# A routed attention and expert kernel: destination column written once, four row buffers, query mask on ACT, keys and context remainder fused on DVE

## What is computed

```python
x = x + xattn(layernorm(x), ctx)      # 16 heads of 16, keys and values from ctx; blocks of 64 queries see their own 64 keys
x = x + ffn(layernorm(x))

def ffn(x):
    weights = softmax(x @ gate_w.T + expert_bias)          # 8 experts
    top_w, top_i = top_k(weights, 2); top_w = top_w / (sum(top_w) + 1e-6)
    out = sum over e of sparse_w[e] * (gelu(x @ w_up[e].T) @ w_down[e].T)      # width 1024
    return layernorm(out) + x
```

## Time and profile before

| What | us |
|---|---|
| median of 3 runs | 847.35 (847.29 to 849.61) |
| the profiled execution, its time | 847.34 |
| its span, first to last instruction | 845.5 |
| outside the span | 1.84 |

### The profile page before, as it was taken

One profiled execution on the slowest core, in us unless ns is written; L12 is line 12 of the kernel. 1 busy time (PEld: TensorE's weight loads), 2 busy tenths in 40 slices (PEclk: granted clock), 3 DMA queues, 4 the chain that ended last, 5 costly groups with the idle time before them and its releaser, 6 DMA issues.

```text
span 845.5 us, 19594 instructions
## 1 busy us (share of the span) xinstructions
PE 731.7 (87%) x6084; PEld 661.2 (78%) x6084; DVE 568.6 (67%) x1356; ACT 355.6 (42%) x651; POOL 408.2 (48%) x629
## 2 busy tenths in 40 slices
PE   4999999989899883059659999999999999999990
PEld 4899999889788873048548999999989889999980
DVE  4899999999989983068145555555666667766662
ACT  2777777667566651022112222222333334433441
POOL 3676776557688876644363111111233335433353
PEclk9999999999999997569888999999999999999995
DMA  4333333233345433443742111112222233333222
GB/s 157 101 101 103 111 104 113 88 88 107 125 132 144 125 100 112 122 133 103 194 124 85 51 51 50 39 48 69 82 88 88 82 93 105 107 95 94 83 89 93
DMA packets 61785, 84.17 MB, mean 100 GB/s; under 512 B 7232, under 2 KB 52672, under 8 KB 61696
## 3 DMA queue, kind: packets, MB, share of 16 engines
q1 hardware_dynamic: 54016, 62.98, 25.8%
q0 software_dynamic: 6816, 18.65, 6.1%
q10 hardware_dynamic: 864, 1.36, 0.5%
HBM read 53.56 MB, written 29.40 MB: 98 GB/s over the span
## 4 chain that ended last, share of the span: by engine, by line
PE 41%; issue 23%; POOL 20%; DVE 7%; DMA 5%; SPq 2%; ACT 0%; POOLq 0%; DVEq 0%; ACTq 0%
PE ps_a L578 11%; PE ps_b L594 10%; POOL y_rows L1176 6%; POOL x_sorted L1100 4%; PE ps_a L453 4%; PE ps_b L496 3%; PE ps_a L533 2%; PE ps_c L475 2%; PE ps_c L480 2%; POOL tiny L1163 2%; PE ps_b L463 2%; DMA x_sorted<-area,slot_row 2%; PE ps_a L518 2%; POOL weights_s L1144 1%; DMA area<-xn_rows 1%
## 5 line engine op out<-in xcount | busy, mean ns | idle before, releaser
L578 PE MATMUL ps_a<-area,weights_s 128*128 128x256 f16 x1872 | 217.3, 277 | 1.6 <-DVE area L909 1.6
L594 PE MATMUL ps_b<-weights_s,area 128*128 x1872 | 210.6, 273 | 0.6 <-issue 0.6
L578 PEld LDWEIGHTS ps_a<-area,weights_s 128*128 x1872 | 185.8, 99 | 26.3 <-issue 2.8
L594 PEld LDWEIGHTS ps_b<-weights_s,area 128*128 128x128 f16 x1872 | 183.1, 98 | 22.1 <-issue 0.9
L1176 POOL DMA_INDIRECT y_rows<-weights_s,tiny x78 | 85.7, 1099 | 128.6 <-ACT weights_s L1065 100.9
L1058 ACT ACTIVATE area<-ps_a 128x512 f32<-128x512 f32 x156 | 92.6, 597 | 119.7 <-PE ps_a L578 119.0
L945 DVE SCALAR_TENSOR_TENSOR area<-area 128x512 f16<-128x512 f32 x156 | 108.1, 693 | 5.3
L1065 ACT ACTIVATE weights_s<-ps_b 128x512 f32<-128x512 f32 x39 | 23.3, 599 | 197.5 <-PE ps_b L594 165.4
L1100 POOL DMA_INDIRECT x_sorted<-area,slot_row x64 | 69.5, 1087 | 63.3 <-POOL area L1096 45.8
L943 DVE TENSOR_SCALAR area<-area 128x512 f16<-128x512 f32 x156 | 67.2, 430 | 23.6 <-ACT area L1058 22.5
L907 DVE TENSOR_SCALAR area<-ps_c 128x512 f16<-128x512 f32 x39 | 26.9, 689 | 79.1 <-PE ps_c L561 78.9
(11 more groups left out here) (149 smaller groups left out, 1158.3 us busy)
## 6 DMA issues: line engine op xcount, KB each, us to landing
weights_s<-weights SPq DMA_DIRECT2D x32, 512.0 KB, 3.6
area<-x_sorted SPq DMA_DIRECT2D x39, 257.0 KB, 2.9
area<-xn_rows SPq DMA_DIRECT2D x64, 128.0 KB, 2.5
area<-y_rows SPq DMA_DIRECT2D x32, 256.0 KB, 2.9
resid<-x_in SPq DMA_DIRECT2D x32, 128.0 KB, 2.2
area<-ctx_t SPq DMA_DIRECT2D x32, 128.0 KB, 2.0
xn_rows<-area SPq DMA_DIRECT2D x32, 128.0 KB, 1.7
out<-resid SPq DMA_DIRECT2D x32, 128.0 KB, 2.8
```

The source lines that it names most:

```text
L578: mm = pe.matmul(ps_h[:, q, (ic % 2) * SLOTS:(ic % 2 + 1) * SLOTS], weights_s[:, bass.ds(first + ((2 * hc + part) * WCOLS + ic * P), P)], ...
L594: mm = pe.matmul(ps_y[:, b, v * D:(v + 1) * D], g[b][:, ic, v * P:(v + 1) * P], weights_s[:, bass.ds(first + (col + part * WCOLS), D)], st ...
```

## The change

The destination column is no longer written into each buffer by POOL. `xn_rows` becomes twice 4096 rows of 257 columns; its last column is filled once from a constant by one DMA on ACT's queue at the start; SP stores each tile's rows twice; a row load brings all 257 columns. POOL's scatter waits for the load alone. There are four row buffers, and `spill` is read from the constants. The distribution of the scatters over the steps is new: one tile each in steps 22 to 34 (0 to 12), two each in steps 35 and 36 (13 to 16); tiles 17 to 21 come after the steps on POOL, and on SP after item 2.

The query operand is written by ACT out of PSUM with mask as scale and masked bias as bias, in four operations of 128 x 128, behind L1010 and ahead of the exponential; `q_b` is gone. The key operand is written by DVE in two fused operations over all 128 partitions with a strip mask, which wait for the four query operations; the zeros at the start are gone. The context's remainder is one fused DVE operation behind the keys, and the scaling of the context goes into ACT's rounding operation and into this one.

```diff
-RING = 3
+RING = 4
...
+    r[:, R_AT:R_END] = SLOTS + p[:, None] + P * np.arange(TOPK * TILES)[None]
...
-        xn_rows = nc.dram_tensor("xn_rows", [TOKENS, D], F32, kind="Internal").ap()
+        xn_rows = nc.dram_tensor("xn_rows", [TOPK * TOKENS, ROW], F32, kind="Internal").ap()
...
-            if i < 32:
+            if i < 35:
                 return (i - 22,)
-            return (10,) if i == 32 else (2 * i - 55, 2 * i - 54)
+            return (2 * i - 57, 2 * i - 56)
...
             def row_in(n):
                 for m, s, uses in loads_of(n):
                     since(sp, rsc[s], 16 * uses)
+                    if m == 0:
+                        sp.wait_ge(at_out, 16)
                     sp.wait_ge(xn2_out[n % 2], 16 * (n // 2 + 1))
-                    sp.dma_start(xr[s][:, 0:D], xn_rows[n * P:(n + 1) * P, :]).then_inc(rin[s], 16)
+                    sp.dma_start(xr[s], xn_by_tile[n + m % TOPK * TILES]).then_inc(rin[s], 16)
...
-                    sp.dma_start(xn_rows[bass.ds(t * P, P), :], xn2).then_inc(xn2_out[b], 16)
+                    sp.dma_start(xn_by_tile.rearrange("(c t) p d -> t p c d", c=TOPK)[bass.ds(t, 1), :, :, 0:D].rearrange("a p c d -> p (a c) d"),
+                                 xn2.unsqueeze(1).to_broadcast([P, TOPK, D])).then_inc(xn2_out[b], 16)
...
-                for n in {-3: (19, 20, 21), -1: (22, 23), 0: (24, 25, 26), 1: (27, 28, 29, 30, 31)}.get(k, ()):
+                for n in {-2: (17, 18, 19, 20, 21), -1: (22, 23), 0: (24, 25, 26), 1: (27, 28, 29, 30, 31)}.get(k, ()):
                     row_in(n)
...
-                    pe.wait_ge(q_r, t + 1)
-                    pe.wait_ge(k_r, STRIPS * (t + 1))
+                    pe.wait_ge(q_r, 2 * HC * (t + 1))
+                    pe.wait_ge(k_r, HC * (t + 1))
...
-                                           k_bd[:, c, n].rearrange("p s k -> p (s k)"), start=True, stop=True)
+                                           k_bd[:, c, :, n * BLOCK:(n + 1) * BLOCK], start=True, stop=True)
...
-            dve.memset(k_bd.rearrange("p c b s k -> p (c b s k)"), 0.0).then_inc(zeroed, 1)
...
                 t, half, b = here(j, u, 1)
                 if valid(t):
                     dve.wait_ge(k_ps, t + 1)
-                    since(dve, q_r, t)
-                    dve.tensor_tensor(q_b, ps_q, bq_s.unsqueeze(2).to_broadcast([P, HC, P]), ALU.add).then_inc(qb_r, 1)
-                    for s in range(STRIPS):
-                        r = slice(32 * s, 32 * s + 32)
-                        dve.tensor_tensor(k_bd[r, :, :, s, :], ps_k[r].rearrange("p c (b k) -> p c b k", b=NB),
-                                          bk_s[r].unsqueeze(2).unsqueeze(3).to_broadcast([32, HC, NB, BLOCK]), ALU.add).then_inc(k_r, 1)
+                    dve.wait_ge(q_r, 2 * HC * (t + 1))
+                    since(dve, s_ps, t)
+                    for c in range(HC):
+                        dve.scalar_tensor_tensor(k_bd[:, c], ps_k[:, c].unsqueeze(1).to_broadcast([P, SIDE, P]), bk_s[:, c:c + 1],
+                                                 cst[:, C_STRIP:C_STRIP + SIDE].unsqueeze(2).to_broadcast([P, SIDE, P]),
+                                                 ALU.add, ALU.mult).then_inc(k_r, 1)
+
+                t, half, b = here(j, u, 0)
+                if valid(t):
+                    dve.wait_ge(ctx_hi_r, t + 1)
+                    since(dve, v_ps, t)
+                    dve.scalar_tensor_tensor(ctx_lo, ctx[b], CTX_SCALE, ctx_hi, ALU.mult, ALU.subtract).then_inc(ctx_lo_r, 1)
...
-            act.dma_start(rc, route_consts).then_inc(rc_in, 16)
+            act.dma_start(rc, route_consts[:, 0:R_AT]).then_inc(rc_in, 16)
+            act.dma_start(xn_rows.rearrange("(g p) d -> p g d", p=P)[:, :, D:ROW], route_consts[:, R_AT:R_END].unsqueeze(2),
+                          allow_slow_non_contiguous=True).then_inc(at_out, 16)
...
-                    act.wait_ge(ctx_in[b], 16 * (half + 1))
-                    act.wait_ge(k_ps, t + 1)
-                    act.activation(ctx[b], ctx[b], ACT.Copy, scale=CTX_SCALE).then_inc(ctx_scaled, 1)
...
-                    act.wait_ge(ctx_scaled, t + 1)
+                    act.wait_ge(ctx_in[b], 16 * (half + 1))
                     since(act, v_ps, t)
-                    since(act, ctx_lo_r, t)
-                    act.activation(ctx_hi, ctx[b], ACT.Copy).then_inc(ctx_hi_r, 1)
+                    act.activation(ctx_hi, ctx[b], ACT.Copy, scale=CTX_SCALE).then_inc(ctx_hi_r, 1)
...
+                t, half, b = here(j, u, 1)
+                if valid(t):
+                    if isinstance(t, int) and t == 0:
+                        act.wait_ge(bqm_r, 1)
+                    act.wait_ge(k_ps, t + 1)
+                    since(act, s_ps, t)
+                    for c in range(HC):
+                        for h in range(2):
+                            act.activation(q_m[:, c, :, h, :], ps_q[:, c].rearrange("p (b q) -> p b q", b=NB), ACT.Identity,
+                                           bias=bq_m[:, c, h:h + 1], scale=cst[:, C_MASK + h:C_MASK + h + 1]).then_inc(q_r, 1)
...
                 for m, s, uses in loads_of(n):
-                    since(pool, rsc[s], 16 * uses)
-                    pool.tensor_scalar(xr[s][:, D:ROW], rc[:, R_P1:R_P1 + 1], float(SLOTS - 1 + n * P + m % TOPK * TOKENS), None,
-                                       ALU.add).then_inc(col_r, 1)
                     pool.wait_ge(rin[s], 16 * (uses + 1))
-                    pool.wait_ge(col_r, m + 1)
...
-                    pool.tensor_tensor(ctx_lo, ctx[b], ctx_hi, ALU.subtract).then_inc(ctx_lo_r, 1)
...
-                    pool.tensor_tensor(q_m.rearrange("p c b h q -> p (c b) h q"),
...
```

More of the change, by code:

```diff
@@ L30 @@
 STRIPS = 4
+SIDE = STRIPS
 NB = P // BLOCK
@@ L73, in constants @@
     c[:, C_MASK:C_MASK + 2] = (p[:, None] // DK % 2) == np.arange(2)[None]
+    c[:, C_STRIP:C_STRIP + SIDE] = (p[:, None] // (2 * DK) % SIDE) == np.arange(SIDE)[None]
     halves = lambda v: np.ascontiguousarray(v.astype(np.float16)).view(np.float32)
@@ L117, in program @@
         gate_bias = cst[:, C_GATE_B:C_END]
-        AREA = 10415
+        AREA = 10416
         area = sb("area", [P, AREA])
@@ L184, in program @@
         item_col = carve(1)
[L185 removed]
+        rc = carve(R_AT)
         tri16, ones16 = (rc[:, n:n + P // 2].bitcast(F16) for n in (R_TRI, R_ONES))
+        spill = rc[:, R_SPILL:R_SPILL + SUBS]
         r_desc, r_row, r_item = (rc[:, n:n + E] for n in (R_DESC, R_ROW, R_ITEM))
@@ L252, in program @@
         xt_ps, xt_r = sem("xt_ps"), sem("xt_r")
-        wv_scaled, wv_hi_r, wv_lo_r, ctx_scaled, ctx_hi_r, ctx_lo_r = (
-            sem(n) for n in ("wv_scaled", "wv_hi_r", "wv_lo_r", "ctx_scaled", "ctx_hi_r", "ctx_lo_r"))
-        q_r, qb_r, k_ps, k_r, v_ps, v_r = (sem(n) for n in ("q_r", "qb_r", "k_ps", "k_r", "v_ps", "v_r"))
+        wv_scaled, wv_hi_r, wv_lo_r, ctx_hi_r, ctx_lo_r = (
+            sem(n) for n in ("wv_scaled", "wv_hi_r", "wv_lo_r", "ctx_hi_r", "ctx_lo_r"))
+        bqm_r, q_r, k_ps, k_r, v_ps, v_r = (sem(n) for n in ("bqm_r", "q_r", "k_ps", "k_r", "v_ps", "v_r"))
         s_ps, max_r, sub_r, p_r, pt_ps, pt_r = (sem(n) for n in ("s_ps", "max_r", "sub_r", "p_r", "pt_ps", "pt_r"))
@@ L354, in _ @@
         def _(sp):
+            xn_by_tile = xn_rows.rearrange("(g p) d -> g p d", p=P)
             def row_in(n):
@@ L470, in step @@
                     pe.wait_ge(xt_r, t + 1)
-                    since(pe, qb_r, t)
-                    since(pe, k_r, STRIPS * t)
+                    since(pe, q_r, 2 * HC * t)
+                    since(pe, k_r, HC * t)
                     for c in range(HC):
@@ L890, in _ @@
             dve.wait_ge(small_in, 16)
+            dve.tensor_tensor(bq_m, bq_s.unsqueeze(2).to_broadcast([P, HC, 2]), cst[:, C_MASK:C_MASK + 2].unsqueeze(1).to_broadcast([P, HC, 2]),
+                              ALU.mult).then_inc(bqm_r, 1)
             step(-1, 1)
@@ L987, in step @@
                 if valid(t):
-                    act.wait_ge(ctx_in[b], 16 * (half + 1))
-                    act.wait_ge(k_ps, t + 1)
-                    act.activation(ctx[b], ctx[b], ACT.Copy, scale=CTX_SCALE).then_inc(ctx_scaled, 1)
-                t, half, b = here(j, u, 0)
-                if valid(t):
                     act.wait_ge(w_in[b], 16 * (half + 1))
@@ L1121, in step @@
                     pool.tensor_tensor(r, r, bo_s, ALU.add).then_inc(bo_added, 1)
-                t, half, b = here(j, u, 0)
-                if valid(t):
-                    pool.wait_ge(ctx_hi_r, t + 1)
-                    since(pool, v_ps, t)
-                    pool.tensor_tensor(ctx_lo, ctx[b], ctx_hi, ALU.subtract).then_inc(ctx_lo_r, 1)
-                t, half, b = here(j, u, 1)
-                if valid(t):
-                    if isinstance(t, int) and t == 0:
-                        pool.wait_ge(small_in, 16)
-                    pool.wait_ge(qb_r, t + 1)
-                    since(pool, s_ps, t)
```

(6 more changed lines are left out.)

29 lines of the change are left out of this document (12 added, 17 removed).

## The result

The changed kernel takes 877.31 us (median of 4 runs, 874.23 to 884.34), the kernel before 847.32 beside it: 1.036 times as long, interval 1.0331 to 1.039. The forecast was 856, its range ended at 874: the sign was right and the size wrong by 21 us. The profiled execution took 874.23, its span 872.4 against 845.5. It is the fastest of the four and lies 3 us under the median; the other three show a mean granted clock of TensorE of 0.938 to 0.946 against its 0.948.

The account below looks back on a forecast made before the run. TensorE was taken to bound early steps, POOL the scatter steps, SP and POOL together the time behind attention. From 847.34 us, +35.2 attention, -16.9 and -10.2 tail, +1 column gave 856; range 838 to 874.

Parts of the forecast that it names:

- What bounds the kernel: Early steps are TensorE's, scatter steps POOL's, then SP and POOL together; from item 6 the last 401 us stay the same.
- The stall, 1.82 a step: Every attention step: TensorE waits 1.82 us before L518 for DVE's context remainder behind the keys; period 10.52 instead of 8.70.
- No stall: Rival, attention steps: ACT and DVE finish before L518, so steps stay 8.70 and the time is 799; chance 0.06.
- the routing work I count at nothing more: Steps 15 to 21: DVE's routing work adds nothing, hidden by DVE's new waits for the queries.
- the +0.3 of steps 22 to 30: Former POOL-bound scatter steps take 94.7 us against 94.4, limited by L518 instead of POOL.
- +7.6: Steps 15 to 21, with routing work on DVE: seven steps of 10.52 take 73.6 us against 66.0.
- The prediction's own case without that cover: Steps 15 to 21: if DVE's waits don't hide the routing work, 66.0 grows by 7 x 1.82, 5 us more.
- neither bound (+18, +55): Attention steps: limits of the predicted +35.2 us, said to come from stall bounds of 1.25 and 2.40 a step.
- The tail: Behind attention: item 0 starts 16.9 us earlier against attention's end; four row buffers save 10.2 more up to item 6.
- POOL keeps its wait: Rival, scatters: the 0.79 us ahead of each is its own, so one stays near 1.9; time 872, chance 0.07.
- The tail repays the stall: Rival, row buffers between attention and item 6: quicker buffer turns make the kernel not slower; 845 us, chance 0.22.
- The column write is slow: Rival, starting column DMA: at 390 ns an element it holds SP's queue at step 22; 876 us, chance 0.05.

Follow-up runs that it names:

- Experiment 1: Changed kernel with DVE making the context remainder right behind the subtraction of the row maximum, ahead of rows and keys: 871.41 us, ratio 1.0287.
- experiment 3: Changed kernel with the products of probabilities and values made twice: 870.01 us, 1.0308; also with POOL's weight remainder waiting for DVE's xn2: 861.87 us, 1.021.
- the filled kernel: Changed kernel with TensorE's products of probabilities and values made twice in each step, writing the same numbers: 870.01 us, ratio 1.0308.
- experiment 5: Changed kernel with the column DMA issued twice at the start, the second into a tensor nobody reads; SP's first row load waits for both: 887.66 us, 1.0491.
- experiment 6: Changed kernel, remainder first, POOL's weight remainder behind xn2, `o_t` ahead of the exponential: 822.99 us, 0.9732; also x's load ahead of xn2's store: 814.99 us, 0.9627.
- POOL's wait: Changed kernel with POOL's weight remainder started only after DVE has written xn2: 871.95 us, 1.0328; also with TensorE's probability-value products made twice: 861.87 us, 1.021.

## Why the prediction came out as it did

- **What bounds the kernel.** Right. A wait put into the early steps was paid in full in each, and item 6 to the end kept its 401 us.
- **The stall, 1.82 a step.** Right in its place, links and size: ordinary steps take 10.44 to 10.53 against 10.52 predicted. Experiment 1 shows the remainder's place as the cause: with the remainder first the wait ahead of the value product is gone. "No stall" (799) falls.
- **The step that failed:** "the routing work I count at nothing more, since DVE's new waits for the queries hide it", and with it the +0.3 of steps 22 to 30, which took every step at a flat 10.52. The waits do hide the routing work itself, such as the 1.3 us of tile 17: without the follow-ups of experiment 3 the two terms are +8.3 and +1.3. But DVE's rows end before those waits, and 0.23 us behind them stands POOL's weight remainder. Routing work that moves the rows by more than that doesn't cost its own length but POOL's whole operation, 2.2 for 0.41. In tiles 15 to 22 this and the clock made +12.8 of +7.6, and in 22 to 31 +7.5 of +0.3. The prediction's own case without that cover, 7 x 1.82 or 12.7, meets the +12.8 by number only.
- **Why it wasn't seen.** The sum had POOL's two operations go ("POOL sheds its two tensor operations") and asked only what that frees, not what now starts earlier: L1142, from 1.55 behind the rows to 0.23. The Trainium skill, "SBUF — State Buffer", "Who interferes with whom", says that VectorE's tensor_scalar in its two-port modes and GpSimd share a port pair as a lock, so that the later one waits for the whole of the earlier. The rows agree in the length: 2.22 beside 2.23, 2.29 beside 2.12. They don't show the order, for in the second DVE's row begins 0.01 us ahead of POOL's and is the long one all the same, and no run here shows the mode that the operation runs in.
- **A stall was priced as idle time alone.** Waiting TensorE also lost clock: 0.96 in the steps against 0.99 before, 6.5 us by the filled kernel. No term of the sum had it, and neither bound (+18, +55) was worked out from it; that +50.1 lies under +55 is luck. With the prediction's own upper stall of 2.40 its terms add to +53, not +55.
- **The tail.** Right: -15.5 for -16.9 and -8.6 for -10.2. Scatters follow each other by 1.26 with 0.30 idle (1.36 predicted), so "POOL keeps its wait" (872) falls. Item 0 to 6 took 74.7 for 73.1. "The tail repays the stall" (845) would have needed a quicker tail than this and no follow-ups.
- **The column.** The count was right: 9072 packets on ACT's queue (q10) for 864, so 8208 more. They land 19.1 us after issue (below). "The column write is slow" (876) names nearly the measured time by a cause that isn't there: SP needs it 200 us later. The sum's +1 for it came out by luck: the 1.1 at the start is that of the queries and keys (experiment 5). By the Trainium skill, "DMA: Bandwidth & Descriptors", "Rules for kernel authors", one descriptor per element was to be expected of a strided last dimension, and the count agrees.

```profile
q10 hardware_dynamic: 9072, 1.39, 1.8%
...
xn_rows<-route_consts ACTq DMA_DIRECT2D x1, 32.0 KB, 19.1
```

- **The doubled store, nothing.** Right for the changed kernel, where the stall covers it (DVE waits 0.8 us in all for x). Without that cover x is late by up to 2.1 us in alternate steps, as experiment 6 shows, for its load stands behind the store. That the doubling makes it late is argued from the store's median landing of 3.8 us, 1.7 before; a single store was not run with these moves.
- **The range.** 838 to 874 against 877.31. Its upper end came from the scatter rival, which didn't come true, not from the attention, which held the risk.

What stays open: how much of the 12.6 us each follow-up has on its own, and why the clock fell in just the steps it did (10 and 25 had no meeting, and steps with as much waiting kept 1.00).

## What to carry to other kernels

When an edit takes work off an engine, look at what that engine does next and against whom it will now run: here the freed POOL moved a 2.1 us operation next to DVE's rows. When an edit adds a wait ahead of TensorE, price the idle time and the clock. Put the operation that the critical engine waits for ahead of those that wait themselves; then look again, for each repair here showed the next late one.

## What the runs showed of the hardware

- A DVE operation of 0.41 us on 128 x 256 f32 took 2.2 to 2.3 where POOL's 128 x 1024 subtraction ran beside it, and in the rows shown ended 0.16 us behind it. DVE's keys out of PSUM (1.41 us for two, 149.94 to 151.35) ran beside the same POOL operation (148.80 to 150.93) at no loss; in the step of tile 17, behind it, they took 1.40.
- A second DMA of 8192 elements on one queue held ACT's list for 13.81 us at its issue, the first 0.69.
- Run with POOL's wait, TensorE with 16 matmuls more in each step (as the profile counts them) finished the kernel sooner (861.87 us at 1.021 against 871.95 at 1.0328).
